# Second pass of a six-layer decoder: rounding of the gated rows on ScalarE instead of VectorE, the residual sum beside the token transpose, and a new order of steps

## What is computed

```
x = _layernorm(x + _L0_xattn_ref(x, ctx_1024, ...))      # 16 heads of 16, 77 context keys
x = _layernorm(x + _L0_ffn_ref(x, w_gate, w_up, w_down)) # 256 -> 1024 -> 256
...
def _act_quant(x):
    scale = 127.0 / jnp.clip(jnp.max(jnp.abs(x), axis=-1, keepdims=True), 1e-05)
    xq = jnp.clip(jnp.round(x * scale), -128.0, 127.0) / scale
    return x + jax.lax.stop_gradient(xq - x)
def _bitlinear(x, w):
    return jnp.einsum('bsi,oi->bso', _act_quant(x), _weight_quant(w))
...
gate = jax.nn.silu(_bitlinear(x, w_gate))
up = _bitlinear(x, w_up)
return _bitlinear(gate * up, w_down)
```

## Time and profile before

| | |
|---|---|
| time of the profiled execution | 6723.68 us |
| its span in the trace | 6721.6 us |
| pass A, first to last instruction | about 45 to 1260 us |
| pass B | about 1284 to 3184 us |
| busy over the span: PE, DVE, ACT, POOL | 85%, 80%, 57%, 38% |
| mean granted clock of TensorE over the span | 0.926 of full |

### The profile page before, as it was taken

One profiled execution on the slowest core, in us unless ns is written; L12 is line 12 of the kernel. 1 busy time (PEld: TensorE's weight loads), 2 busy tenths in 40 slices (PEclk: granted clock), 3 DMA queues, 4 the chain that ended last, 5 costly groups with the idle time before them and its releaser, 6 DMA issues. The chain is left out here.

```text
span 6721.6 us, 142690 instructions
## 1 busy us (share of the span) xinstructions
PE 5683.2 (85%) x54804; PEld 3882.5 (58%) x54914; DVE 5399.0 (80%) x12498; ACT 3825.4 (57%) x7089; POOL 2562.5 (38%) x2572
## 2 busy tenths in 40 slices
PE   6999999687878878886899999999139888988988
PEld 4666666454545455553676677766126666666665
DVE  6878888588888888888787887888668888888887
ACT  5777777455555555553566666666325555555554
POOL 0122111122222222222354445444126666666665
PEclk9999999788888898987999999999569999999998
DMA  1111111100000000000011001100100000000000
GB/s 58 43 44 44 46 44 41 36 20 22 23 21 25 21 21 25 21 20 24 26 33 32 30 25 34 31 30 28 36 22 23 23 25 27 21 27 23 23 23 18
DMA packets 140390, 194.38 MB, mean 29 GB/s; under 512 B 25808, under 2 KB 63696, under 8 KB 139344
## 3 DMA queue, kind: packets, MB, share of 16 engines
q1 hardware_dynamic: 139728, 185.26, 8.7%
HBM read 113.03 MB, written 72.18 MB: 28 GB/s over the span
## 5 line engine op out<-in xcount | busy, mean ns | idle before, releaser
L1085 DVE TENSOR_REDUCE Amp<-pj 128x2 f32<-128x512 f32 x1024 | 644.6, 683 | 118.2 <-PE pj L800 118.2
L1085 DVE TENSOR_REDUCE Dmp<-pj 128x2 f32<-128x512 f32 x1024 | 641.1, 684 | 88.4 <-PE pj L800 86.4
L1085 DVE TENSOR_REDUCE Cmp<-pj 128x2 f32<-128x512 f32 x1024 | 642.8, 685 | 82.1 <-PE pj L800 80.9
L938 ACT ACTIVATE Dpr<-st 128x512 f32<-128x512 f32 x1024 | 529.2, 606 | 312.8 <-PE st L735 311.7
L938 ACT ACTIVATE Apr<-st 128x512 f32<-128x512 f32 x1024 | 528.6, 603 | 274.3 <-PE st L735 272.6
L938 ACT ACTIVATE Cpr<-st 128x512 f32<-128x512 f32 x1024 | 528.7, 603 | 174.6 <-PE st L735 172.6
L1020 POOL TENSOR_SCALAR Bve<-Bmv 128x2 f32<-128x2 f32 x128 | 29.1, 227 | 1339.4 <-DVE Bmv L1152 1339.4
L996 POOL TENSOR_TENSOR Dnrm<-Dnrm,power 128x32 f32<-128x32 f32 x64 | 348.8, 5449 | 196.5 <-DVE Dnrm L1063 196.5
L1020 POOL TENSOR_SCALAR Ave<-Amv 128x2 f32<-128x2 f32 x64 | 14.6, 228 | 1020.2 <-DVE Amv L1152 1020.2
L938 ACT ACTIVATE Bpr<-st 77x512 f32<-77x512 f32 x512 | 261.5, 592 | 191.7 <-PE st L735 191.0
L735 PE MATMUL st<-Aq,Ak 32*128 32x256 f32 x4096 | 330.4, 397 | 5.6 <-DVE Aq L1092 4.7
(11 more groups left out here) (310 smaller groups left out, 15553.9 us busy)
## 6 DMA issues: line engine op xcount, KB each, us to landing
Ax0T<-in_xT SPq DMA_DIRECT2D x64, 256.0 KB, 2.8
Ax<-in_x SPq DMA_DIRECT2D x64, 256.0 KB, 3.4
x_A_scratch<-Ax SPq DMA_DIRECT2D x64, 256.0 KB, 2.0
Bx<-x_A_scratch SPq DMA_DIRECT2D x64, 256.0 KB, 2.9
x_B_scratch<-Bx SPq DMA_DIRECT2D x64, 256.0 KB, 2.0
Cx<-x_B_scratch SPq DMA_DIRECT2D x64, 256.0 KB, 2.9
x_C_scratch<-Cx SPq DMA_DIRECT2D x64, 256.0 KB, 2.0
Dx<-x_C_scratch SPq DMA_DIRECT2D x64, 256.0 KB
```

The lines of the kernel that those rows point to most:

```text
L938: ck.tell(act.activation(dst, st[bank][0:n, :], ACT.Exp, scale=HD ** -0.5), "probs_ready", step)
L1085: ins = dve.tensor_reduce(dst, src, AX.X, ALU.max, negate=True)
```

## The change

Three things change in pass B, and nothing elsewhere but two constants in the setup. ScalarE does both halves of the rounding in `hq`, by two Identity activations over 128x1024 with the row's scale and the magic number as per-partition operands; VectorE still finds the maximum and the scales and then signals `scale_ready`. The clip at 127 is left out. In `fq` two small VectorE instructions become one. The residual sum moves from the step `norm` 0 to the step `xT`, and the loads wait for it there. The order string and `AHEAD` are replaced.

```diff
-    return {"A": ("v", "A1", s), "B": ("norm", "A2", s, 0), "C": ("norm", "A3", s, 0),
+    return {"A": ("v", "A1", s), "B": ("xT", "B", s), "C": ("norm", "A3", s, 0),
...
-    "B": ("303232331303231030120310322321303033312131331212320130213111122013221223021132020133002211"
+    "B": ("333101332320211321033220030121333111113023212330223320233211220312021120231320012012011300"
...
-AHEAD = {"A": (8, 4, 1, 0), "B": (21, 21, 30, 32), "C": (33, 33, 28, 13), "D": (32, 33, 10, 21)}
+AHEAD = {"A": (8, 4, 1, 0), "B": (30, 26, 32, 32), "C": (33, 33, 28, 13), "D": (32, 33, 10, 21)}
...
-        "hq": ["dve_step"] * 6 + ["hq_ready"],
+        "hq": ["dve_step"] * 3 + ["scale_ready", "hid_rounded", "hq_ready"],
...
                         elif phase == "B":
-                            ck.wait("base_ready", ("norm", "A2", s, 0))
+                            ck.wait("base_ready", ("xT", "B", s))
...
+                    elif kind == "hq":
+
+                        t = step[3]
+                        flat = hid[s][:].rearrange("p a b -> p (a b)")
+                        ck.wait("scale_ready", step)
+                        ck.tell(act.activation(flat, flat, ACT.Identity, scale=qsc[s][:, t, 11:12], bias=rounding[:, 0:1]),
+                                "hid_rounded", step)
+                        if t > 0:
+                            ck.wait("hqT_ready", ("hT", att, s, t - 1))
+                        ck.wait("hid_rounded", step)
+                        ck.tell(act.activation(hq[s][:], flat, ACT.Identity, bias=rounding[:, 1:2]), "hq_ready", step)
...
+                    elif kind == "xT" and att == "B":
+                        ck.wait("x_ready", ("ln", "F", s))
+                        ck.wait("xT_ready", step)
+                        ck.tell(pool.tensor_tensor(res[s][:], x0[s][:], row["A2_bo"][:].unsqueeze(1).to_broadcast([P, QT, D]),
+                                                   ALU.add), "base_ready", step)
...
-                        link(ck, dve.tensor_scalar(qsc[s][:, :, 5:6], qsc[s][:, :, 1:2], wq_inv[:, 1:2], 1.0 / QMAX,
-                                                   ALU.mult, ALU.mult))
-                        ck.tell(dve.tensor_tensor(qsc[s][:, :, 6:7], qsc[s][:, :, 4:5], qsc[s][:, :, 5:6], ALU.mult),
-                                  "xq_ready", step)
+                        ck.tell(dve.scalar_tensor_tensor(out=qsc[s][:, :, 6:7], in0=qsc[s][:, :, 4:5], scalar=wq_up[:],
+                                                         in1=qsc[s][:, :, 1:2], op0=ALU.mult, op1=ALU.mult), "xq_ready", step)
...
-                        link(ck, dve.tensor_scalar(q[:, 11:12], q[:, 9:10], q[:, 6:7], QMAX, ALU.mult, ALU.mult))
-                        link(ck, dve.tensor_scalar(q[:, 10:11], q[:, 8:9], wq_inv[:, 2:3], 1.0 / QMAX,
-                                                   ALU.mult, ALU.mult))
-                        link(ck, dve.tensor_scalar(flat, flat, q[:, 11:12], MAGIC, ALU.mult, ALU.add))
-                        if t > 0:
-                            ck.wait("hqT_ready", ("hT", att, s, t - 1))
-                        ck.tell(dve.tensor_scalar(hq[s][:], flat, MAGIC, QMAX, ALU.subtract, ALU.min), "hq_ready", step)
-                        ck.wait("hq_ready", step)
+                        dve.tensor_scalar(q[:, 11:12], q[:, 9:10], q[:, 6:7], QMAX, ALU.mult, ALU.mult)
+                        ck.tell(dve.tensor_scalar(q[:, 10:11], q[:, 8:9], wq_inv[:, 2:3], 1.0 / QMAX,
+                                                  ALU.mult, ALU.mult), "scale_ready", step)
+                        ck.wait("scale_ready", step)
```

More of the change, by code:

```diff
@@ L189 @@
           "303133122203303333"),
-    "B": ("303232331303231030120310322321303033312131331212320130213111122013221223021132020133002211"
-          "03230210203310200012131202230101001022032012010101"),
+    "B": ("333101332320211321033220030121333111113023212330223320233211220312021120231320012012011300"
+          "21000310302310122001320123012030232031010110320132"),
     "C": ("331000033303002311021020103223303010330233030013000202213012312101013001231220011133311103"
@@ L253, in signals @@
         "norm": ["dve_step", "normed"] + ["x_used"] * (att == "A1" and step[-1] == 1)
-        + ["base_ready"] * (att != "A1" and step[-1] == 0),
+        + ["base_ready"] * (att in ("A3", "A4") and step[-1] == 0),
         "oT": ["attnT_ready"],
@@ L258, in signals @@
         "ln": ["dve_step", "var_ready", "pool_step", "pool_step", "x_ready"],
-        "xT": ["xT_ready"],
-        "fq": ["dve_step"] * 8 + ["xq_ready"],
+        "xT": ["xT_ready"] + ["base_ready"] * (att == "B"),
+        "fq": ["dve_step"] * 7 + ["xq_ready"],
         "xqT": ["xqT_ready"],
         "gu": ["tanh_ready", "gated", "hid_ready"],
-        "hq": ["dve_step"] * 6 + ["hq_ready"],
+        "hq": ["dve_step"] * 3 + ["scale_ready", "hid_rounded", "hq_ready"],
         "hT": ["hqT_ready"],
@@ L383, in build @@
         power = sb("power", [P, QT * H])
+        rounding = sb("rounding", [P, 2])
+        wq_up = sb("wq_up", [P, 1])
         twice = sb("twice", [P, S])
@@ L415, in _ @@
                 pool.memset(ones_b[:], 1.0)
+                pool.memset(rounding[:, 0:1], MAGIC)
+                pool.memset(rounding[:, 1:2], -MAGIC)
                 pool.memset(power[:], -0.5).then_inc(setup_pool, 1)
@@ L454, in _ @@
                 link(dve.reciprocal(wq_inv[:], small[:, 6:9]))
+                link(dve.tensor_scalar(wq_up[:], wq_inv[:, 1:2], 1.0 / QMAX, None, ALU.mult))
                 for i, q in enumerate((wg, wu, wd)):
@@ L1005, in do @@
                         ck.tell(pool.tensor_tensor(qr4, qr4, emb, ALU.add), "rotated", step)
-                    elif kind == "norm" and att != "A1" and step[3] == 0:
+                    elif kind == "xT" and att == "B":
[3 more added lines that the diff above has]
+                                                   ALU.add), "base_ready", step)
+                    elif kind == "norm" and att in ("A3", "A4") and step[3] == 0:
                         bias = row[att + "_bo"][:].unsqueeze(1).to_broadcast([P, QT, D])
@@ L1011, in do @@
                         else:
-                            if att == "A2":
-                                ck.wait("x_ready", ("ln", "F", s))
-                            ck.wait("xT_ready", ("xT", phase, s))
+                            ck.wait("xT_ready", ("xT", "C", s))
                         ck.tell(pool.tensor_tensor(res[s][:], (x if att == "A4" else x0)[s][:], bias, ALU.add),
@@ L1111, in do @@
                         bank = ck.bank(step)[:].rearrange("p (t d) -> p t d", t=QT)
-                        ck.wait("base_ready", ("norm", att, s, 0))
+                        ck.wait("base_ready", ("xT", "B", s) if att == "A2" else ("norm", att, s, 0))
                         if att == "A4":
```

## The result

The changed kernel takes 6689.78 us (median of five, 6686.91 to 6695.42) against 6723.12 us of the kernel before: a ratio of 0.995, 95% interval 0.9937 to 0.9963. It is faster by 33 us, where 149 us were forecast (6574 us). The direction and the range held; the size was off by more than a factor of four.

What follows compares the result with a forecast made beforehand. Pass B was taken to be set by VectorE with short waits, TensorE close behind. Between 212 and 114 us saved, the middle 163 less 16 for the late load gave 147 us, forecast 6574 us, range 6450 to 6712 us.

Steps and rivals of the forecast that it cites:

- the late load: Pass B: stream 2's load behind stream 3's store may make TensorE wait; bounds 0 and 64 us, 16 us taken.
- the fifteen steps: Pass B: TensorE's steps from stream 3's layer norm to `k` of stream 2, of 140 in a round; about 12.7 us.
- the rival of the lumps: Pass B: grouped attentions and feed-forwards take nearly all the gain, attention clock staying 0.87; about 6640 to 6705 us, chance 0.15.
- the first range: The forecast's own case, between the two ends: 6540 to 6630 us, chance 0.49.
- VectorE's relief: Pass B: rounding moved off VectorE (185 us), merged `fq` instruction (11) and removed gaps (16) relieve it of 212 us.
- ScalarE in the chain: Rival, pass B: nothing gained and each of 128 roundings lengthens its chain by 859 ns; 110 us, 6831 us, chance 0.03.
- The new order: Pass B: groups the four attentions and the four feed-forwards, and removes the cause of VectorE's largest wait, for `Bx`.
- the sum by halves: Pass B: VectorE's feed-forward 57 us plus TensorE's attention 54.6 us, without overlap 111.6 us a round, pass 1786 us.
- the middle: Pass B: 163 us saved, between 212 us with waits unchanged and 114 us with the halves fully apart.
- The moved sum: Pass B: residual sum, 80.3 us of GpSimd, moved and not removed; up to 81 us if cover were gone, 0 taken.
- The clock rival: Pass B: TensorE half idle in the feed-forward half drops to 1.2 GHz; 1995 us for the pass, 6819 us, chance 0.09.

Runs made afterwards that it cites:

- the kernel with the loads first: The changed kernel with pass B's order string edited so the four loads stand ahead of every store in the round: 6585.14 us, ratio 0.9789 to the kernel before.

## Why the prediction was wrong

**The step that failed** is the late load: "the bounds are 0 and 4 us a round (64 us); I take 1 us a round, 16 us, since the margin is mostly there". The mechanism was the right one, in the right place. Measured, it is 105 us, 89 us more than taken and 41 above my own upper bound. Four things were wrong in it, and the round shown above has them in numbers. GpSimd starts there on the layer norm of stream 3 at

```profile
1858.32 0.23 POOL L1039 TENSOR_SCALAR Bve<-Bmv 128x2 f32<-128x2 f32 x1 [24.48 <-DVE Bmv L1171]
```

From there to `k` of stream 2 at 1868.18 it is 9.9 us and not 6.6: the prediction said "besides the issues" and then left them out, and from the issue of the store to that of the last load they are 2.8 us. TensorE was ready for `k` at 1863.97 (the end of the queries' products), 5.7 us behind GpSimd's start; the 12.7 us for the fifteen steps were an average over the round. The difference is the wait of 4.2 us, and it was 4.1 to 5.9 us in every round, where my upper bound was 4. Third, the bound counted the wait alone, not the slower products around it (34 us in all). And I took a value near the lower end without a reason from the trace. Without this step the forecast would have been 6574 - 16 = 6558 us; the kernel with the loads first, where the term is gone, takes 6585.

Of the signs that the prediction named for being wrong, this one was there: TensorE waits 4.7 us a round for the DMA of `Bx`, where more than 1 us was to count. The time of 6690 us also lies where the rival of the lumps has it (6640 to 6705 us), but not by its mechanism: with the lumps as they are and the loads first, the time is 6585 us, inside the first range.

**VectorE's relief**, 212 us, of which 196 were busy time and 16 gaps: measured 216 us of busy time between the two kernels, and 235 us of busy time for 232 us of time when only the code differs in the new order with the loads first. The new instructions were foreseen at 1197 and 1110 ns, and took, in the changed kernel,

```profile
L973 ACT ACTIVATE Bhid<-Bhid,rounding,Bqsc 128x1024 f32<-128x1024 f32 x128 | 157.8, 1233 | 72.9 <-DVE Bqsc L1212 72.9
L978 ACT ACTIVATE Bhq<-Bhid,rounding 128x1024 bf16<-128x1024 f32 x128 | 146.9, 1148 | 8.3 <-ACT Bhid L973 0.4
```

The merged instruction of `fq` took 222 ns, inside the bounds of 165 and 273.

**ScalarE in the chain.** I gave this rival 0.03 and priced it at 110 us. In the changed order it did not come, and VectorE shows no wait for ScalarE's `Bhq`, as predicted. But in the old order the rounding costs 400 us. My price counted only the longer chain of a row, 859 ns; the real mechanism is the queue. Here the rule of the Trainium skill (ScalarE: Activation LUTs, Rules for kernel authors) that additions and multiplications belong on VectorE holds for the old order and fails in the new one with the loads first, and what decides it is what stands behind the instruction, not its length.

**The new order.** The lumps were foreseen, and the sum by halves was near: 111.6 us a round for halves fully apart, (1900 - 212) / 16 = 105.5 for none of it, and the middle, 108.6, taken. The kernel with the loads first has 1757 / 16 = 109.8. That it is so near is in part luck: the middle was a choice between two ends and not worked out, and two misses partly cancel. The order cost 90 us with the old code, where the middle allows it 212 - 163 = 49, and the code gave 232, where 212 were counted. The picture behind it was too simple. Two 10 us stretches of the changed kernel, one in each half:

```profile
1870.00:1880.00 10.00, 9.00 (x75) 7.08 (x74) 4.60 (x13) 6.09 (x11) 3.05 (x4) 0.89 0.00 0
...
1940.00:1950.00 10.00, 9.00 (x42) 3.10 (x42) 9.65 (x18) 5.71 (x8) 3.40 (x4) 0.80 0.00 0
```

VectorE is 46% busy in the first, 97% in the second, so the halves are real. In the attention half what was taken from TensorE came off (14 of 14 us, a small test near the noise). In the feed-forward half only a part did, whichever engine was relieved (17 of 68 us from VectorE, 25 of 74 from TensorE), so that half has no single bound; the order interlocks three engines there. It stays open why VectorE's relief by the rounding came off in full. That the rounding sat on the same engine and in the same half as the maximum, of which only a quarter came off, suggests that the first microseconds taken from VectorE count fully and later ones do not; no run here shows where that ends.

**The moved sum**, priced at nothing, seems worth about 12 us in the new order and costs 48 in the old. The clock rival (slower by half speed through the feed-forward half) did not happen; the granted clock there was 0.71 to 0.95 by stretches of 10 us in the round shown, against 0.89 to 1.00 in its attention half. What this clock cost in the feed-forward half no run separates.

## What to carry to other kernels

In an order written by hand, an edit and the order made for it are one change: here the code alone loses 428 us, the order alone 181 us, and together they gain 33. Before moving work to an idle engine, read what will stand behind it in that engine's queue. And when an order moves DMA issues, look for a load behind a store: the wait is shown at the first instruction that needs the load, while the cost shows on two other engines. Here the places of three digits in the string were worth three times the whole change.

Before counting what an edit takes from TensorE, read its busy time with and without: durations of single products overlap, and their sum (60 us for the bias products) can be four times what the engine loses (14 us).

## What was not expected of the hardware

A VectorE instruction of two elements per partition took five times as long beside a GpSimd instruction. With the sum at `norm` 0 in the changed kernel, GpSimd makes two sums in a row, and once in each round a small VectorE instruction falls beside their start and takes 1.21 us instead of 0.22. GpSimd, then VectorE, in that kernel:

```profile
2039.75 2.50 POOL L1031 TENSOR_TENSOR Bres<-Bx,A_bo 128x512 f32<-128x512 f32 x2
```

```profile
2039.83 1.21 DVE L1185 SCALAR_TENSOR_TENSOR Bqsc<-Bqsc,wq_up 128x2 f32<-128x2 f32 x1
2044.10 0.22 DVE L1185 SCALAR_TENSOR_TENSOR Bqsc<-Bqsc,wq_up 128x2 f32<-128x2 f32 x1
```

The mean of these instructions is 470 ns there and 222 ns with the sum at `xT`. Over the pass, 23 us of VectorE's busy time went with the move, more than the 12 us by which the kernel became faster. The slow instruction ends at 2041.04, about when the first of the two sums does (2039.75 and 1.27 us for one), as if it had waited for that sum to finish. That the two share something is argued from these times; no run here separates it.
